# Adapter attention: the mask laid by 32 rows in three bf16 parts, written by four column tiles of PE into the banks of both passes

## The reference

```python
scores = jnp.einsum('bhqd,bhkd->bhqk', q, k) * inv_sqrt_d
scores = scores + attention_mask
scores = jnp.maximum(scores, jnp.finfo(scores.dtype).min)
w = jax.nn.softmax(scores.astype(jnp.float32), axis=-1).astype(q.dtype)
attn_output = jnp.einsum('bhqk,bhkd->bhqd', w, v)
...
a_scores = jnp.einsum('bhqd,bhkd->bhqk', q, a_k) * inv_sqrt_d
a_scores = jnp.tanh(gate) * jax.nn.softmax(a_scores.astype(jnp.float32), axis=-1).astype(q.dtype)
attn_output = attn_output + jnp.einsum('bhqk,bhkd->bhqd', a_scores, a_v)
```

## Time and profile before

| | us |
|---|---|
| median of 3 runs | 1192.85 (1191.91 to 1195.93) |
| span of the profiled execution (the profile gives no other time for it) | 1193.7 |
| PE busy | 1128.8 (95%) |
| PE weight loads busy | 934.4 (78%) |
| DVE busy | 993.6 (83%) |
| ACT busy | 660.4 (55%) |
| POOL busy | 656.9 (55%) |

### The profile page before, as it was taken

The page is one execution under the profiler, slowest core; times in us unless marked ns, Lnnn a source line. Parts: engine busy times, 40 slices in busy tenths (PEclk is TensorE's granted clock), DMA queues, the critical chain, the costliest instruction groups (busy, mean ns, idle before and its releaser), DMA issues.

```text
span 1193.7 us, 29551 instructions
## 1 busy us (share of the span) xinstructions
PE 1128.8 (95%) x11172; PEld 934.4 (78%) x11172; DVE 993.6 (83%) x2284; ACT 660.4 (55%) x1687; POOL 656.9 (55%) x706
## 2 busy tenths in 40 slices
PE   5899999899999999879999999999999999999997
PEld 5667666666776766546899899998999899997887
DVE  6768887888889898978888888888888888877977
ACT  5466554566766667565555444444444444558663
POOL 4467655545455455254778544544554454847665
PEclk9899999999999999999999999999999999999999
DMA  6875443334333433212222000000000100101111
GB/s 161 205 186 135 122 125 87 87 95 116 88 106 101 106 97 97 76 58 76 68 63 63 1 1 2 1 1 2 1 1 1 37 1 1 37 18 37 36 36 36
DMA packets 98670, 76.68 MB, mean 64 GB/s; under 512 B 73547, under 2 KB 86987, under 8 KB 98529
## 3 DMA queue, kind: packets, MB, share of 16 engines
q1 hardware_dynamic: 98529, 74.80, 23.1%
HBM read 53.86 MB, written 19.92 MB: 62 GB/s over the span
## 4 chain that ended last, share of the span: by engine, by line
PE 58%; DVE 23%; issue 7%; ACT 5%; POOL 3%; SPq 2%; DMA 2%; DVEq 0%; POOLq 0%; ACTq 0%
PE bank L1518 5%; DVE B_nr L737 4%; PE bank L1519 4%; PE bank L1520 4%; PE bank L1574 4%; PE bank L1547 4%; PE bank L611 4%; DVE PT L746 3%; PE bank L472 2%; PE bank L554 2%; SPq L1154 2%; PE bank L1534 2%; PE bank L1589 2%; PE bank L1587 2%; PE bank L1588 2%
## 5 line engine op out<-in xcount | busy, mean ns | idle before, releaser
L1822 POOL TENSOR_TENSOR C_QK<-C_t1b,C_t2b 128x512 f32<-128x512 f32 x128 | 168.9, 1320 | 226.6 <-DVE C_t2b L1661 226.0
L1658 DVE SCALAR_TENSOR_TENSOR C_t1b<-bank,C_bcol,C_tabs 64x512 f32<-64x512 f32 x256 | 192.0, 750 | 37.3 <-PE bank L1520 33.2
L737 DVE TENSOR_REDUCE B_nr<-bank 128x4 f32<-128x512 f32 x256 | 164.4, 684 | 22.6 <-PE bank L554 21.0
L1518 PE MATMUL bank<-C_XTh,C_Wh 128*128 128x512 f32 x256 | 111.9, 437 | 4.4 <-DVE C_t2b L1661 1.9
L985 ACT ACTIVATE PT<-bank 128x512 f32<-128x512 f32 x160 | 92.2, 598 | 39.8 <-PE bank L589 39.3
L1754 ACT ACTIVATE C_P<-bank,C_nm 128x128 f32<-128x128 f32 x256 | 90.7, 367 | 34.0 <-DVE C_nm L1671 32.4
L978 ACT ACTIVATE PT<-PT 128x512 f32<-128x512 f32 x96 | 59.3, 630 | 88.7 <-DVE PT L746 88.7
L1773 ACT ACTIVATE C_V<-bank 128x512 f32<-128x512 f32 x64 | 38.1, 597 | 124.1 <-PE bank L1536 122.5
L611 PE MATMUL bank<-PT,vpool 128*32 128x128 f32 x2048 | 97.4, 285 | 4.3 <-ACT PT L978 3.1
L1519 PE MATMUL bank<-C_XTl,C_Wh 128*128 128x512 f32 x256 | 101.2, 395 | 0.0
L1520 PE MATMUL bank<-C_XTh,C_Wl 128*128 128x512 f32 x256 | 100.8, 394 | 0.0
(11 more groups left out here) (267 smaller groups left out, 3683.5 us busy)
## 6 DMA issues: line engine op xcount, KB each, us to landing
Adrq<-PB SPq DMA_DIRECT2D x16, 192.0 KB, 3.2
Adrk<-PB SPq DMA_DIRECT2D x16, 192.0 KB, 3.4
stk<-Adrq SPq DMA_DIRECT2D x16, 192.0 KB
stk<-Adrk SPq DMA_DIRECT2D x16, 192.0 KB
Bdrq<-PB SPq DMA_DIRECT2D x16, 192.0 KB, 2.7
stk<-Bdrq SPq DMA_DIRECT2D x32, 96.0 KB
Bdrk<-PB SPq DMA_DIRECT2D x16, 192.0 KB, 2.7
stk<-Bdrk SPq DMA_DIRECT2D x32, 96.0 KB
```

The source lines that it names most:

```text
L737: e.tensor_reduce(dst, bank[n % 2][:, :].rearrange("p (a b) -> p a b", a=4), AX.X, ALU.max, negate=True).then_inc(sem("m_dve"), 1)
L1518: e.matmul(o[:, :], CWh[hp][:, cs], XCh[0][:, t, :], start=t == 0, stop=False)
L1658: e.scalar_tensor_tensor(out=v4(t1b[kq][lo:lo + 64, :]), in0=v4(o[hi:hi + 64, :]), scalar=bc[hi:hi + 64, :], in1=tabsC[hi:hi + 64, 2 * kq ...
L1822: e.tensor_tensor(QK[v % 3][:, kq, :], t1b[kq][:, :], t2b[kq][:, :], ALU.add).then_inc(sem("rc_pool"), 1)
```

## The change

- The clamped mask is split into three bf16 parts (MQ, parts 0 to 2) by ACT and POOL in turn (mask_part, mask_rest; mask_parts gives the steps).
- PE transposes the three parts (six bf16 transposes in mask_parts_turned instead of two of float32), ACT copies them to MTQ.
- SP lays both out anew: mask_rows copies MQ to MP, mask_t_rows copies MTQ to MTP. In MP the partitions 32 j to 32 j + 31 hold part j of the 32 mask rows of group g, for g = 0 to 3 along the free axis. Each of the two takes twelve DMAs of 32 partitions by 512 bytes for a chunk, 24 for a chunk and 192 in all.
- With pick (96 x 32: the 32 x 32 identity three times under each other) as moving partner, mask_by_rows writes the mask into a bank by four column tiles: one matmul of 512 columns and 96 rows for each 32 output rows. It does so in both passes; the products then add to it (`start=False`).
- DVE's mask2 is gone, ACT takes the exponential of masked units straight from the bank, and the bank of pass 2 is free when ACT is done (bank2_free, semaphore e_act).
- From step 64 on, PE's order in a step is the value product, the mask of pass 1, the mask of pass 2, pass 1, pass 2, then the rest.
- Several small semaphores are merged (consts, ld_B), and the reserve `dynamic_dma_scratch_size` is set to 8192, with which the added tiles fit in SBUF.

```diff
+    mask_parts = [{s + k: c for s, c in clamps.items()} for k in (1, 2, 3, 4)]
+    masks_out = {s + 5: c for s, c in clamps.items()}
+    mask_turns = {s + (1 if c < 10 else 3): c for s, (c, _) in masked.items()}
+    masks_t_out = {bg0(c) + 28: c for c in range(8, 16)}
...
+        def mask_by_rows(o, parts, b):
+
+            for g in range(4):
+                e.matmul(o[32 * g:32 * g + 32, :].rearrange("p (a b) -> p a b", a=4), pick[0:96, :],
+                         parts[0:96, g, b, :].unsqueeze(1).to_broadcast([96, 4, 128]), start=True, stop=False, skip_group_check=True)
+
+        def mask1(n):
+            b = unit(n)[1]
+            c = 8 + b // 2
+            if n >= 2:
+                q.wait_ge("m_dve", n - 1)
+            q.wait_ge("consts", 5)
+            q.wait_ge(*parts_ready("mp_in", c))
+            mask_by_rows(bank[n % 2], MP[c % 2], b % 2)
+
+        def mask2(n):
+            b = unit(n)[1]
+            c = 8 + b // 2
+            bank2_free(n)
+            q.wait_ge("consts", 5)
+            q.wait_ge(*parts_ready("mtp_in", c))
+            mask_by_rows(bank2(n), MTP[c % 2], b % 2)
...
-                elif not kd:
-                    q.wait_ge("identr", 1)
-                    q.wait_ge("mkl_pool", b // 2 + 1)
-                    for k, part in enumerate((MKh, MKl)):
-                        e.matmul(scores, identr[:, :], part[(b // 2) % 2][:, b % 2, :].unsqueeze(1).to_broadcast([128, 4, 128]),
-                                 start=k == 0, stop=False, skip_group_check=True)
...
         for s in steps:
+            if s >= NA:
+                for n in pv_units(s):
+                    pv(n)
+                for n in pass1_units(s):
+                    if is_masked(n):
+                        mask1(n)
+                for n in pass2_units(s):
+                    if is_masked(n):
+                        mask2(n)
             if pass1_units(s):
                 pass1(pass1_units(s))
             if pass2_units(s):
                 pass2(pass2_units(s))
-            for n in pv_units(s):
-                pv(n)
+            if s < NA:
+                for n in pv_units(s):
+                    pv(n)
...
-        def mask2(n):
-            L, b, kd, t, i, hs = unit(n)
-            v4 = lambda a: a.rearrange("p (a b) -> p a b", a=4)
-            q.wait_ge("mt_act", b // 2 + 1)
-            q.wait_ge("t_pe", n + 1)
-            q.wait_ge("pv_pe", pt_free(n))
-            e.tensor_tensor(v4(pt_of(n)[:, :]), v4(bank2(n)[:, :]),
-                            MT[(b // 2) % 2][:, b % 2, :].unsqueeze(1).to_broadcast([128, 4, 128]), ALU.add).then_inc(sem("mt_dve"), 1)
...
+        def mask_rows(c):
+
+            q.wait_ge("mq_pool", 2 * (c - 7))
+            if c >= 10:
+                q.wait_ge("s_pe", last_unit(2 * (c - 2) + 1, 0) + 1)
+            for j in range(3):
+                for g in range(4):
+                    load(MP[c % 2][32 * j:32 * j + 32, g, :, :], MQ[32 * g:32 * g + 32, j, :, :], "mp_in")
+
+        def mask_t_rows(c):
+            q.wait_ge("mt_act", c - 7)
+            if c >= 10:
+                q.wait_ge("t_pe", last_unit(2 * (c - 2) + 1, 0) + 1)
+            for j in range(3):
+                for g in range(4):
+                    load(MTP[c % 2][32 * j:32 * j + 32, g, :, :], MTQ[32 * g:32 * g + 32, j, :, :], "mtp_in")
...
             for c, ti, b in stacked.get(s, ()):
                 stack_in(c, ti, b)
+            if s in masks_out:
+                mask_rows(masks_out[s])
+            if s in masks_t_out:
+                mask_t_rows(masks_t_out[s])
             if s in parts:
                 parts_out(*parts[s])
```

More of the change, by code:

```diff
@@ L86, in program @@
     Wl = [sb(f"{L}_Wl", [128, 2, 1024], F32R, st_ab) for L in "AB"]
-    identr = sb("B_identr", [128, 128], F32R, st_ab)
-    MKh = [sb(f"B_MKh{i}", [128, 2, 128], F32R, st_ab) for i in range(2)]
-    MKl = [sb(f"B_MKl{i}", [128, 2, 128], F32R, st_ab) for i in range(2)]
+    MP = [sb(f"B_MP{i}", [128, 4, 2, 128], BF16, st_ab) for i in range(2)]
     nrA = [sb(f"A_nr{i}", [128, 1, 16], F32, st_ab) for i in range(2)]
@@ L100, in program @@
     gt = sb("B_gt", [128, 36], F32, st_ab)
+    pick = sb("B_pick", [128, 32], BF16, st_ab)
+    MQ = sb("B_MQ", [128, 3, 2, 128], BF16, st_ab)
+    MR = sb("B_MR", [128, 2, 128], F32, st_ab)
+    MTP = [sb(f"B_MTP{i}", [128, 4, 2, 128], BF16, st_ab) for i in range(2)]
+    MTQ = sb("B_MTQ", [128, 3, 2, 128], BF16, st_ab)
     tabsA = VPOOL[:, 224:248, :].rearrange("p (t a) b -> p t (a b)", t=6)
@@ L317, in small_products @@
             yield ("pj",) + projs[s]
-        if s in masked:
-            yield "mt", masked[s][0]
+        if s in mask_turns:
+            yield "mp", mask_turns[s]
         if s in vals:
@@ L506, in project, with mask_parts_turned @@
                 m.then_inc(sem("pj_pe"), 1)
[L508 to L512, removed]
+        def mask_parts_turned(c):
+            q.wait_ge("mq_pool", 2 * (c - 7))
+            o = turn(("mp", c), "mt_act", c - 7)[:, :].bitcast(BF16)
+            for part in range(3):
+                for b in range(2):
+                    k = 2 * part + b
+                    m = e.transpose(o[:, k * 128:k * 128 + 128], MQ[:, part, b, :], identb[:, :])
             m.then_inc(sem("mt_pe"), 1)
@@ L588, in pass2 @@
                     rows, h = (slice(64 * t, 64 * t + 54), hs[j] % 16) if L else (slice(0, 99), hs[j])
+                    alone = bool(L) and not is_masked(n)
                     m = e.matmul(bank2(n)[:, j * 128:j * 128 + 128], (AS if kd else KS[L])[i3][rows, h, :], QS[L][i3][rows, h, :],
-                                 start=bool(L), stop=bool(L) or j == 3, skip_group_check=not L)
+                                 start=alone, stop=alone or j == 3, skip_group_check=not alone)
                     if j == 3:
@@ L669, in pe_ab @@
                     project(*projs[s], 1)
-            if s in masked:
-                masks(masked[s][0])
+            if s in mask_turns:
+                mask_parts_turned(mask_turns[s])
             if s in vals:
@@ L840, in dve_ab @@
                 shift_parts(e, q, shifts[s], "sh_dve")
-            for n in pass2_units(s):
-                if n >= NA and unit(n)[2] == 0:
-                    mask2(n)
             if s - 1 in wos and s >= MASK_FIRST:
@@ L1035, in act_ab @@
                 x_high(*xts[s - 1])
-            if s - 1 in masked:
-                masks(masked[s - 1][0])
-                mask_high(masked[s - 1][0])
+            if s - 1 in mask_turns:
+                mask_parts_turned(mask_turns[s - 1])
+            for part in range(2):
+                if s in mask_parts[2 * part]:
+                    mask_part(mask_parts[2 * part][s], part)
             if s - 1 in vals:
@@ L1118, in pool_ab @@
                 add_adapter(tos[s - 2][0])
-            if s - 2 in masked:
-                mask_low(masked[s - 2][0])
+            for part in range(2):
+                if s in mask_parts[2 * part + 1]:
+                    mask_rest(mask_parts[2 * part + 1][s], part)
             for part in range(2):
@@ L1467, in norm_pool @@
     def norm_pool(e, q, c):
-        q.wait_ge("mhalf", 1)
+        q.wait_ge("consts", 2)
         q.wait_ge("cn_bn", 9 * c + 9)
```

98 lines of the change are left out of this document (51 added, 47 removed).

## The result

| | us |
|---|---|
| before, median in the same comparison | 1193.05 |
| after, median of 4 runs | 1292.15 (1289.78 to 1298.01) |
| ratio | 1.083 (1.080 to 1.086) |
| span of the profiled execution after | 1296.2 |

The kernel became slower by 99 us. The forecast was 1234 with a range of 1196 to 1274: the side was right, the size was less than half of what came.

A forecast was written before the change was run, and what follows sets the result against it. PE bounds the kernel before; SP's issue list was to become layer B's bound. The profiled 1193.7 + 44.5 (SP's copies less regained waits) + 3 (head) - 6 (tail) = 1235.2, so a median of 1234 us, range 1196 to 1274.

The forecast's parts named there:

- The rival with tiles one behind another: PE's column tiles run serially, 0.94 us a mask bank, some 190 us in all, near 1385; chance 0.03.
- I take 0.475: SP's price in us for each added copy, bounds 0.34 to 0.77; 24 copies make 11.4 us a chunk.
- 35.3 of waits: SP's waits for POOL and ACT between layer B's batches 1 and 14, which it could take back: 35.3 us.
- The copies are as dear as B_nmT: Rival: each added copy on SP costs 0.77 us, giving 1285 us; chance 0.1.
- PE's order ... I cost it at nothing: PE's new step order in layer B adds nothing, but may eat part of the 2.9 us of DVE waits.
- the fast rival of 1163: SP's issues are cheap and PE and DVE decide: about 30 us faster, 1163 us; chance 0.11.
- I take 6: Gain after layer B's batch 14, where SP is nearly empty: 6 of 7.4 us of PE's waits for DVE.
- which I price at 3: Loss of 3 us from chunk 8's first burst of copies, shortly before layer B's first stacks.
- About 3.5 us: Shortening of a layer B chunk if PE and DVE alone decided: 0.5 from masks plus 2 to 3.
- The six bf16 transposes against two of float32 ... I cost at nothing: PE's extra transposes of the mask parts in each chunk were priced at zero.
- 2 to 3 us that DVE's relief was to bring: Part of PE's 2.9 us of waits for DVE in a layer B chunk, expected to go.
- The rule weighed against the row: The skill's rule makes SP's 24 added issues a chunk no matter; trace rows of 0.65 us an issue were preferred.

The follow-up runs named there:

- e7: e6 with both masks of a step ahead of both passes, value product still last: 1198.14 us, ratio 1.005.
- e2: The changed kernel with mask copies issued for the first two chunks only (48 of 192), new PE order kept: 1244.91 us, ratio 1.043.
- e4: e2 with PE's old order, value product last and each mask ahead of its own pass: 1217.01 us, ratio 1.019.
- e8: The changed kernel with mask parts laid out through DRAM, 64 DMAs in place of 192, new PE order kept: 1229.77 us, ratio 1.031.
- e6: e8 with PE's old order and the mask parts' transposes three steps later in most chunks: 1196.13 us, ratio 1.0025.
- e3: The changed kernel with all 192 copies but PE's old order, value product last: 1286.03 us, ratio 1.076.
- e1: The kernel before plus only the 192 copies, of zeros to a tile nobody reads: 1281.78 us, ratio 1.074.
- e9: Half the change: column-tile mask in pass 1 only, laid out through DRAM, pass 2 and PE's order as before: 1192.77 us, ratio 1.000.
- e5: The kernel before with one edit, layer B's value product ahead of both passes on PE: 1369.39 us, ratio 1.146.

## Why the prediction was right in its side and wrong in its size

**The bound was named rightly.** SP's list became the bound, through B_nmT, at pass 2, with its waits for POOL and ACT used up. DVE's share of a chunk fell under 60% (52%), and in the middle of layer B DVE's relief did not show. The column tiles run side by side: eight mask matmuls, two banks, stand from 348.29 to 348.84, so at most 0.28 us a bank, change of shape included; one behind another, at the 0.235 of the prediction, they would take 1.88. The rival with tiles one behind another falls with that. It had not been ruled out as firmly as the prediction says: the value product's eight matmuls have 1024 columns together, which at 0.235 for 512 would take 0.47 one behind another, and their 0.25 us is only half of that. (In the profile's `96*32 96x512` the 96 x 32 are the loaded weights, so the identity is loaded and the mask's rows stream; the description of the kernels calls the identity the moving partner.)

**The step that failed is the price of a copy, "I take 0.475".** SP's issues of the new copies take 0.655 us in the mean over the middle (168 of them, 110.0 us), with some 0.04 between them 0.70, within the bounds of 0.34 and 0.77 but at their far end. Its own sum, with this price: SP's extra 168 x 0.70 = 117.6, less 35.3 of waits, is +82; measured +85.8. In full, the copies took 110.0, the other issues 3.4 more, the gaps between issues 5.5 more, and the waits 33.1 less (19.8 against 52.9). In a chunk 35.0 + 2.3 + 24 x 0.70 = 54.1; measured 54.8. The mechanism stood; this one term was 38 us too small. The nearest row had been chosen by form (one plain piece in each partition), from a pair of issues with 128 partitions in DRAM loads. The rows of the same list in layer B itself said 0.65 for a stack load and 0.77 for B_nmT, both of which touch SBUF in slices of partitions. I took the row that looked simplest, though these two stood nearer and lay close together.

**"The copies are as dear as B_nmT", chance 0.1, was the case that came near.** With its 0.77 it gave 1285. With the measured 0.70 the prediction's own sum is 1193.7 + 82.3 + 3 - 6 = 1273, just inside the range. The other 23 us of the profiled execution are the head (8.9 more than priced), the tail (10.8) and 3.5 in the middle; that execution is the longest of the four, 5.9 us over their median.

**"PE's order ... I cost it at nothing" was wrong, and hidden.** I had looked for the loop of the maxima, which the order does not lengthen by much (e7: 0.9 us a chunk). I missed that the value product, set first in the step, asks for exponentials of the pair that ACT is working on. That is 4.5 us a chunk (e2 against e4; 4.7 with the turn, e8 against e6). With SP no longer the bound the kernel still takes 1230 (e8): the fast rival of 1163 had no ground, whatever an issue cost. Behind SP's bound it shows only in part, in the tail: there SP is no bound, and the new order has 700 us where the old one has 692 to 693.

**The tail, "I take 6".** With the old order the tail is 692.4 (e4) and 691.7 (e6), 3.7 and 4.4 us less than before: the relief is there, near its size. The change has +4.8, because the order takes about 8 us (700.3 against 692.4, e2 and e4, and against 691.7, e8 and e6).

**The head, "which I price at 3", measured 11.9.** The first burst of copies stands ahead of layer B's first stacks. Part of the 11.9 is not the change's at all: layer B's first store of query parts, ahead of every added DMA, starts at 152.9 us before and at 155.3 after, and anywhere from 151.0 (e3) to 155.8 (e8) in the other kernels. Counted from there, the change loses 9.5 us, e3 9.6, e1, whose copies wait for no mask, 7.2, and e8 with 64 DMAs 2.5. So the copies make some 7 of it, and the 2 above that go with SP's wait for the mask's parts, which the profile gives as 3.3 us in the change and 3.5 in e3.

**"About 3.5 us" a chunk by PE and DVE alone was wrong too.** e6 is that case, and its chunk gains 0.1. The 32 banks cost what 16 pairs of matmuls cost, as priced (8.7 us a chunk, against 9.0 before and 8.5 priced), the changes of tile shape included. What failed is "The six bf16 transposes against two of float32 ... I cost at nothing": with the output's transposes and the wait behind them they take 1.9 us a chunk more in e6 (1.9 in e4 too). Of the 2 to 3 us that DVE's relief was to bring, 1.4 came. In the change itself SP's bound hides both. With both masks together, and so one change for a pair (e7), the chunk is no shorter (43.9).

**The rule weighed against the row.** The trace went with the row. SP's issuing, called "usually small relative to the DMA itself" in the Trainium skill, DMA: Bandwidth & Descriptors, under Issuing engines are not separate DMA queues, is 0.70 us for a copy that lands 1.8 us after its issue. One copy starts every 0.70 us while the ones before it are still under way, so here, with 192 small DMAs more on one list, the issue is the cost: 1282 (e1).

What stays open: why some copies take 0.52 and others up to 1.83 us to issue, with a median of 0.59. And how much e9's form could give if DVE were relieved for some banks of pass 2 and PE kept its old order: this was not tried.

## What to carry to other kernels

Price a step that adds many small DMAs as instructions on the issuing engine's list, at the price of that list's own neighbours, and compare the sum with that engine's waits, which the table of busy times doesn't show. Where two lists bound a stretch, their excesses need not add: here the longer one decided, and the next stood right beneath it, so take away each alone before you say what a part costs. Idle time of the weight loads is not idle time of PE: before you call it a cost, look at PE's own starts. And when a consumer is moved forward within an engine's order, look at how far its producer is behind at that point, not only at the loop you had in mind.

## What the runs showed of the hardware that had not been expected

**The price of an issue does not follow its bytes.** On SP's list in the kernel before, mean duration of the instruction over the middle of layer B: 0.41 us for 128 partitions by 1 KB (the residual's copy), 0.47 to 0.52 for a store of parts, 0.61 for a stack load, 0.73 for B_nmT (3 partitions by 16 pieces); and in the change 0.655 for a copy of 32 partitions by 512 bytes between tiles in SBUF. Form alone doesn't fix it either: the residual's copy takes 0.55 in the change. The three loads of e9 that bring 32 partitions by four pieces from DRAM take 1.27 us together in five of eight chunks and 1.73 to 2.76 in the others; with the store before them they are four issues for the layout that takes the change twelve.

**TensorE's granted clock fell where PE waited, and PE's work after the waits took longer.** Four windows of the changed kernel, in which layer B begins:

```profile
226.00:229.00 3.00, 1.94 (x23) 1.20 (x22) 2.76 (x7) 0.95 (x5) 2.94 (x4) 1.00 0.61 127
229.00:232.00 3.00, 2.04 (x18) 1.66 (x18) 2.70 (x5) 1.02 (x6) 1.60 (x7) 0.72 0.46 131
232.00:236.00 4.00, 3.20 (x23) 1.84 (x22) 1.66 (x3) 1.47 (x7) 0.00 (x0) 0.50 0.14 32
236.00:240.00 4.00, 3.53 (x28) 3.37 (x28) 1.61 (x3) 1.08 (x2) 0.00 (x0) 0.50 0.13 28
```

Between 227 and 233 us PE waits 0.84, 1.18 and 0.77 us; from 232 to 240 us the clock is 0.50, the lower level of 1.2 GHz, though PE has work again. Two lines of its timeline, the same eight mask matmuls at 2.4 and at 1.2 GHz:

```profile
226.02 0.62 PE L539 MATMUL bank<-B_MP,B_pick 96*32 96x512 bf16 x8
...
234.93 1.05 PE L539 MATMUL bank<-B_MTP,B_pick 96*32 96x512 bf16 x8
```

Over the whole execution the mean granted clock is 0.990 before, 0.954 after and 0.920 in e5, the kernel in which PE waits most. The prediction had no term for this, and what it adds to the 99 us was not measured by itself.
